# Integer feed-forward layers: exact integer weights, two matmul terms for three, and three steps on other engines

## What is computed

```python
SCALE = 1.0 / 127.0
w = w_int.astype(float32) * SCALE        # w_gate, w_up: 384 x 128, w_down: 128 x 384, integers -127..127
g, u = xn @ w_gate.T, xn @ w_up.T
x = x + (silu(g) * u) @ w_down.T
```

## Time and profile before

| | |
|---|---|
| Runs | 4287.07, 4288.15, 4292.68 us; median 4288.15 |
| Profiled execution | 4286.97 us; span of the records 4285.2 us |
| ffn5 stage: start of the weights' DMA to end of the last statistics | 3685.7 to 3776.2, 90.5 us |
| ffn7 stage, the same | 4183.5 to 4273.8, 90.4 us |
| Busy in the ffn7 stage | TensorE matmuls 66.8, VectorE 62.0, ScalarE 33.9, GpSimd 0.0 us |
| Mean granted TensorE clock in either stage | 0.88 |

### The profile page before, as it was taken

The page is one execution under the profiler, slowest core; times in us unless marked ns, Lnnn a source line. Parts: engine busy times, 40 slices in busy tenths (PEclk is TensorE's granted clock), DMA queues, the critical chain, the costliest instruction groups (busy, mean ns, idle before and its releaser), DMA issues. The chain is left out here.

```text
span 4285.2 us, 58306 instructions
## 1 busy us (share of the span) xinstructions
PE 3440.0 (80%) x18432; PEld 2108.1 (49%) x18432; DVE 3112.8 (73%) x7125; ACT 2445.8 (57%) x4454; POOL 1239.0 (29%) x855
## 2 busy tenths in 40 slices
PE   5788888687946999999999978793499999657736
PEld 2455555365733555555555536572366666433314
DVE  3899999656864777777777745685388887569986
ACT  2788888535722656556565534572299999322203
POOL 0000000034421566666566654341000000025520
PEclk9899999878976999999999988896799999778868
DMA  5333332212436666666766611342634342100000
GB/s 184 60 62 62 62 51 35 37 42 102 143 97 81 86 87 89 85 85 87 90 85 86 84 23 46 112 142 67 189 45 61 60 64 31 26 18 8 5 29 26
DMA packets 285571, 303.79 MB, mean 71 GB/s; under 512 B 97951, under 2 KB 187487, under 8 KB 285140
## 3 DMA queue, kind: packets, MB, share of 16 engines
q1 hardware_dynamic: 275540, 279.07, 37.0%
q0 software_dynamic: 9728, 20.99, 1.4%
HBM read 122.30 MB, written 75.96 MB: 46 GB/s over the span
## 5 line engine op out<-in xcount | busy, mean ns | idle before, releaser
L1118 DVE TENSOR_REDUCE at_b_top<-ps 128x1 f32<-128x512 f32 x1024 | 661.9, 680 | 356.9 <-PE ps L878 356.2
L1007 ACT ACTIVATE at_b_e<-ps 128x512 f32<-128x512 f32 x1024 | 583.6, 598 | 474.2 <-PE ps L884 461.2
L550 ACT ACTIVATE at_a_e<-at_a_logits,at_a_neg_top 128x512 f32<-128x512 f32 x1024 | 656.1, 716 | 156.1 <-DVE at_a_neg_top L610 155.0
L777 POOL TENSOR_TENSOR at_b_e_pair<-at_b_e 128x1024 f32<-128x1024 f32 x256 | 603.8, 2380 | 402.5 <-PE ps L906 400.0
L474 PE MATMUL ps<-at_a_k,at_a_q 96*128 96x512 f32 x1024 | 476.3, 491 | 187.4 <-DVE at_a_clipped L578 118.3
L878 PE MATMUL ps<-at_b_k,at_b_q 96*128 96x512 f32 x1024 | 502.0, 494 | 40.2 <-DMA at_b_k<-at_b_k_hi 37.9
L543 ACT ACTIVATE at_a_eT<-ps 128x512 f32<-128x512 f32 x896 | 461.9, 589 | 0.4
L884 PE MATMUL ps<-at_b_q,at_b_k 98*128 98x512 f32 x1024 | 427.2, 418 | 19.0 <-ACT at_b_e L1007 18.6
L606 DVE CUSTOM_DVE_ANT_0 at_a_logits<-ps,at_a_strip 128x512 f32<-128x512 f32 x512 | 340.3, 688 | 110.7 <-issue 33.1
L474 PEld LDWEIGHTS ps<-at_a_k,at_a_q 96*128 96x128 f32 x1024 | 184.7, 190 | 399.8 <-DVE at_a_clipped L578 208.8
L578 DVE TENSOR_SCALAR at_a_clipped<-ps 128x512 f32<-128x512 f32 x512 | 351.2, 686 | 39.1 <-PE ps L474 38.0
(11 more groups left out here) (333 smaller groups left out, 6451.5 us busy)
## 6 DMA issues: line engine op xcount, KB each, us to landing
moe_stage<-in_moe_w SPq DMA_DIRECT2D x46, 768.0 KB
at_b_q<-at_b_q_hi SPq DMA_DIRECT2D x128, 256.0 KB, 5.2
at_b_k<-at_b_k_hi SPq DMA_DIRECT2D x128, 256.0 KB, 7.7
v<-in_a_va SPq DMA_DIRECT2D x64, 256.0 KB, 3.6
at_a_v<-v SPq DMA_DIRECT2D x64, 256.0 KB, 7.2
at_b_q<-at_b_q_lo SPq DMA_DIRECT2D x64, 256.0 KB, 7.6
at_b_k<-at_b_k_lo SPq DMA_DIRECT2D x64, 256.0 KB, 8.0
slot_rows<-empty_slots SPq DMA_DIRECT2D x44, 288.0 KB, 7.0
```

The source lines that it names most:

```text
L550: act.activation(e[:, j, qb, :], logits[:, j % 2, qb, :], ACT.Exp, bias=neg_top[:, j % 2, qb:qb + 1]).then_inc(exp_done, 1)
L777: pool.tensor_tensor(e_pair[:, j, :, :], e[r][:, j, 0:2, :], e[r][:, j, 2:4, :], ALU.add).then_inc(pair_done, 1)
L1007: act.activation(e[r][:, j, b, :], g.ps[:, ST_BANK + b % 2, :], ACT.Exp).then_inc(exp_done, 1)
L1118: dve.tensor_reduce(top[:, t, j, qb:qb + 1], g.ps[:, bank, :], AX_X, ALU.max).then_inc(max_done, 1)
```

## The change

`swiglu` becomes `integer_swiglu`, for these two layers alone.

- Weights: the integers, converted to float32 and rounded to float32r, which holds them exactly; no w_lo. Each product takes two matmuls (w on high, w on low), not three.
- 1/127 goes on results: as the scale of Silu, as the scalar of the multiply that makes h, as the scale of the acc copy.
- Normalising moves from VectorE to ScalarE, as x * rstd + shift, with shift = -mean * rstd computed once on VectorE (as `linear_attention` does, L1397 and L1491). In step s it comes last, for batch s+1.
- The acc copy moves from VectorE to ScalarE, at q = 2 as before.
- h_lo of chunk 1 moves from VectorE to GpSimd; chunks 0 and 2 stay.
- The turns of x and of the result get PSUM banks of their own (0 and 1); the turn of x waits for x_lo of the batch before, no longer for `out_added`.

TensorE's order stays. The core of the diff:

```diff
-def swiglu(nc, g, name, packed, E, C, stats, router=None):
+def integer_swiglu(nc, g, name, packed, stats):
...
-                def three(bank, w0, cols, hi, lo, start, stop):
-
-                    pe.matmul(bank, w_hi[:, w0, cols], hi, start=start, stop=False)
-                    pe.matmul(bank, w_lo[:, w0, cols], hi, start=False, stop=False)
-                    return pe.matmul(bank, w_hi[:, w0, cols], lo, start=False, stop=stop)
+                def two(bank, cols, hi, lo, start, stop):
+
+                    pe.matmul(bank, w[:, cols], hi, start=start, stop=False)
+                    return pe.matmul(bank, w[:, cols], lo, start=False, stop=stop)
...
+                def turn_x(n):
+                    pe.wait_ge(xn_done, TB * n)
+                    wait(pe, x_lo_done, n - 1)
...
+                for s in range(1, B + 4):
+                    if inside(s - 1):
+                        pe.wait_ge(x_lo_done, s - 1)
+                        if s - 1 == 1:
+                            pe.wait_ge(w_done, 1)
+                    for q in range(C):
+                        if inside(s - 1):
+                            gate_up(s - 1, q)
+                        n, c = (s - 1, q - 2) if q >= 2 else (s - 2, q + 1)
+                        if inside(n):
+                            down(n, c)
+                        if q == 1 and inside(s):
+                            turn_x(s)
+                        if q == 0 and inside(s - 3):
+                            turn_out(s - 3)
...
+                def normalise_on_act(n):
+                    wait(act, xp_ready, n - 1)
+                    for tb in range(TB):
+                        t = (n - 1) * TB + tb
+                        act.activation(xn[:, tb, :], g.x_all[:, t, :], ACT.Identity, bias=shift[:, t:t + 1],
+                                       scale=g.rstd[:, t:t + 1]).then_inc(xn_done, 1)
+
+                act.wait_ge(shift_done, 1)
+                normalise_on_act(1)
+                act.wait_ge(w_float, 1)
+                act.activation(w[:], stage_f[:], ACT.Copy).then_inc(w_done, 1)
+                for s in range(1, B + 4):
+                    for q in range(C):
+                        if inside(s - 1):
+                            m = nth(s - 1, q)
                             act.wait_ge(gu_ready, m)
                             wait(act, h_done, m - 2)
+                            act.activation(gate[:, m % 2, :], g.ps[:, G_BANK + m % 2, :], ACT.Silu, scale=SCALE
+                                           ).then_inc(gate_done, 1)
+                        n, c = previous(s, q)
+                        if inside(n):
+                            act.wait_ge(h_done, nth(n, c))
+                            wait(act, down_done, nth(n - 1, c))
+                            act.activation(h_hi[:, c, :], h[:, c, :], ACT.Copy).then_inc(h_hi_done, 1)
+                        if q == 1 and inside(s):
+                            act.wait_ge(xp_ready, s)
+                            wait(act, gu_ready, C * (s - 2))
+                            act.activation(x_hi[s % 2][:], g.ps[:, X_BANK, :], ACT.Copy).then_inc(x_hi_done, 1)
+                        if q == 2 and inside(s - 2):
+                            act.wait_ge(down_done, C * (s - 2))
+                            wait(act, out_ready, s - 3)
+                            act.activation(acc[:], g.ps[:, D_BANK + s % 2, :], ACT.Copy, scale=SCALE).then_inc(acc_done, 1)
+                        if q == 2 and s < B:
+                            normalise_on_act(s + 1)
+
+            @block.gpsimd
+            def _(pool):
+                for n in range(1, B + 1):
+                    pool.wait_ge(h_hi_done, nth(n, 1))
+                    pool.tensor_tensor(h_lo[:, 1, :], h[:, 1, :], h_hi[:, 1, :].bitcast(F32), ALU.subtract
+                                       ).then_inc(h_lo1_done, 1)
...
+                            dve.scalar_tensor_tensor(h[:, q, :], g.ps[:, U_BANK + m % 2, :], SCALE, gate[:, m % 2, :],
+                                                     ALU.mult, ALU.mult).then_inc(h_done, 1)
+                        n, c = previous(s, q)
+                        if inside(n) and c != 1:
+                            dve.wait_ge(h_hi_done, nth(n, c))
+                            dve.tensor_tensor(h_lo[:, c, :], h[:, c, :], h_hi[:, c, :].bitcast(F32), ALU.subtract
+                                              ).then_inc(h_lo_done, 1)
```

More of the change, by code:

```diff
@@ L1730, in _ @@
                         dve.tensor_tensor(x, x, yn[:, (b - 1) % 2, :, :], ALU.add).then_inc(added, 1)
-def swiglu(nc, g, name, packed, E, C, stats, router=None):
-    EC = E * C
+def integer_swiglu(nc, g, name, packed, stats):
+    C = HID // P
     W = 3 * C * P
[L1741 to L1746, removed]
+    SCALE = float(np.float32(1.0 / 127.0))
     with Phase(nc, name) as ph:
[L1748 to L1751, removed]
+        stage = ph.sb("stage", [P, W], I32)
+        stage_f = ph.sb("stage_f", [P, W])
+        w = ph.sb("w", [P, W], F32R)
+        shift = ph.sb("shift", [P, TILES])
         xn = ph.sb("xn", [P, TB, DM])
-        xT = ph.sb("xT", [P, S])
         x_hi = [ph.sb(f"x_hi{r}", [P, S], F32R) for r in range(2)]
@@ L1768, in swiglu @@
[L1768 to L1797, removed]
@@ new lines, in integer_swiglu, with nth, inside, previous @@
+        out_ready, out_added, stats_done = (ph.sem(k) for k in ("out_ready", "out_added", "stats_done"))
+        X_BANK, OUT_BANK, G_BANK, U_BANK, D_BANK = 0, 1, 2, 4, 6
+        def nth(n, c):
+            return C * (n - 1) + c + 1
+        def inside(n):
+            return 1 <= n <= B
+        def previous(s, q):
+            return (s - 1, q - 1) if q else (s - 2, C - 1)
+        def wait_low(eng, n, c):
+            if c == 1:
+                wait(eng, h_lo1_done, n)
+            else:
+                wait(eng, h_lo_done, 2 * (n - 1) + (1 if c == 0 else 2))
@@ L1831, in _ @@
[L1831 to L1841, removed]
+                sp.dma_start(stage[:], packed[0]).then_inc(w_loaded, 16)
@@ L1855, in gate_up @@
+                def gate_up(n, c):
+                    m, r = nth(n, c), n % 2
                     wait(pe, gate_done, m - 2)
                     wait(pe, h_done, m - 2)
[L1857 to L1866, removed]
-                    if c == 0:
[L1868 to L1871, removed]
@@ L1927, in _, with down @@
-                run_steps(pe, B, 3, step, U=2)
+                    two(g.ps[:, G_BANK + m % 2, :], slice(c * P, (c + 1) * P), x_hi[r][:], x_lo[r][:], True, True)
+                    two(g.ps[:, U_BANK + m % 2, :], slice((C + c) * P, (C + c + 1) * P), x_hi[r][:], x_lo[r][:],
+                        True, True).then_inc(gu_ready, 1)
+                def down(n, c):
+                    wait_low(pe, n, c)
+                    if c == 0:
+                        wait(pe, acc_done, n - 2)
+                    two(g.ps[:, D_BANK + n % 2, :], slice((2 * C + c) * P, (2 * C + c + 1) * P), h_hi[:, c, :],
+                        h_lo[:, c, :], c == 0, c == C - 1).then_inc(down_done, 1)
@@ new lines, in turn_x, with turn_out @@
+                def turn_x(n):
+                    pe.wait_ge(xn_done, TB * n)
+                    wait(pe, x_lo_done, n - 1)
+                    for tb in range(TB):
+                        ins = pe.transpose(g.ps[:, X_BANK, tb * P:(tb + 1) * P], xn[:, tb, :], g.ident[:])
+                    ins.then_inc(xp_ready, 1)
+                def turn_out(n):
+                    pe.wait_ge(acc_done, n)
+                    wait(pe, out_added, n - 1)
+                    for tb in range(TB):
+                        ins = pe.transpose(g.ps[:, OUT_BANK, tb * P:(tb + 1) * P], acc[:, tb * P:(tb + 1) * P], g.ident[:])
+                    ins.then_inc(out_ready, 1)
```

257 lines of the change are left out of this document (30 added, 227 removed).

## The result

The changed kernel takes 4243.91 us (4236.86 to 4245.00, four runs), the one before 4288.2: ratio of the runs 0.9891 (the two medians alone give 0.9897), 95% interval 0.9874 to 0.9908. The direction was right, the size 1.4 times the forecast.

A forecast was written before the change was run, and what follows sets the result against it. No engine full; a loop of waits through VectorE's queue sets the pace. Stage 7.3 + 11.2 + 40.0 + 16.1 = 74.6 us for 90.4; both stages save 31.6, so 4288.15 - 31.6 = 4256.6 us, range 4245 to 4271.

The forecast's parts named there:

- The loop of the steady step: Silu, h_hi, acc, four normalisings, next Silu, h, h_lo, down matmuls, turn of x, gate and up: 7.2 us a step.
- Start: Stage start, weights' DMA to first matmul: 10.3 us becomes 7.3.
- the rival of the table: ScalarE: normalising function not in Silu's table, loads of 1.28 us on the loop, 4298.7 us in all; chance 0.03.
- the two prices: GpSimd's subtraction: 1.27 us, taken, or 2.19 beside VectorE's scans on SBUF tiles, making its loop 6.5 or 7.45 us.
- three low stretches: TensorE's clock in the six steps of a stage: three drops instead of two, each 1.3 us, +3.9 us.
- the rival to which I gave 0.15: Steady steps: loop faster than the sum, no low stretch of the clock at all, 4248.8 us; chance 0.15.
- the end: From the eighth turn of x to the end of the last statistics: 16.1 us for 17.1.
- first steps: From the first matmul to the third turn of x: 12.6 us becomes 11.2.
- the five steps: Third to eighth turn of x: 36.1 us, with the clock 40.0, for 50.4.
- Clock lost for good: TensorE falls to 1.2 GHz throughout, about 9.2 us a step, each stage saves 4.7, 4278.8 us; chance 0.10.
- GpSimd meeting VectorE: GpSimd's subtraction takes 2.19 us, VectorE's h_lo stretches: +0.25 to +0.75 on twelve steps, 4259.6 to 4265.6 us; chance 0.15.

The follow-up runs named there:

- the split: Changed kernel with ScalarE's four normalisings split, two at the end of a step and two behind h_hi at q = 0 of the next: 4227.81 us, ratio 0.9876 to before.
- two terms alone: Kernel before with the matmul on the weights' low half left out of each product, w_lo still formed: steps 9.06 us at the full clock.
- spread_gaps: Changed kernel with four spare 128x512 copies a step added on ScalarE, results unused: steps 7.73 us behind a first of 8.3.
- split_norm_no_gpsimd: Changed kernel with the four normalisings split over two steps and h_lo of chunk 1 back on VectorE: ratio 0.9878 to the kernel before, stages 64.7 and 64.5 us.
- banks_alone: Kernel before with only separate PSUM banks for the turns of x and of the result, and their waits: ffn7 stage 77.8 us, ffn5 78.3.
- undo_two_terms: Changed kernel with w_lo (zero here) formed again and the third matmul back in each product: steps 7.89 us, ffn7 stage 76.3, ffn5 77.7.
- undo_banks: Changed kernel with both turns in one PSUM bank and the turn of x waiting for the addition to x, done ahead of x_lo: ffn7 stage 78.0 us.

## Why the prediction was off

**Right, with its size.** The loop of the steady step: 7.19 against 7.12 us measured, through the very instructions named. It held under eight edits, to 0.1 us in the steps named: 6.6 (6.65 measured) without acc, 6.5 (6.54) without normalising, 6.53 (6.50) and 6.35 (6.36 in the first steps) with the split, 7.8 (7.89) with three matmuls, 8.9 (8.9) with one bank, 9.1 (9.06) for two terms alone, 7.1 (7.12) without GpSimd. It missed spread_gaps by 0.4 and the later steps of split_norm_no_gpsimd by 0.15, where another loop took over; for banks_alone it gave only a range. Start: 7.3 against 6.9 in ffn7; the conversion of the weights began 0.4 sooner after their issue (3.64 against 4.09 us). That is scatter and not the change: over all profiles it took 3.6 to 4.8 us, and in ffn5 the start took 7.4. Silu of chunk 0 follows the fourth normalising with no gap. GpSimd, Silu's table and the length of a normalising, from the line view and the view by groups:

```profile
L1858 ACT ACTIVATE ffn_gate<-ps x48: 577/597/599, 3699.7 to 4224.8; 128x512 f32<-128x512 f32 x48
L1858 ACT ACT_TABLE_LOAD  x2: 1283/1283/1283, 3698.3 to 4171.5; - x2
```

```profile
L1845 ACT ACTIVATE ffn_xn<-x_all,ffn_shift,rstd 128x128 f32<-128x128 f32 x32 | 13.1, 485 | 61.3 <-DVE ffn_shift L1885 61.3
L1880 POOL TENSOR_TENSOR ffn_h_lo<-ffn_h,ffn_h_hi 128x512 fp32r<-128x512 f32 x8 | 10.2, 1273 | 119.1 <-ACT ffn_h_hi L1864 119.1
```

Normalising 485 ns each. One table load a stage: the rival of the table is out, and the rule that the prediction took from the Trainium skill (ScalarE: Activation LUTs, Table sets: the hidden batching unit) agrees with the trace. GpSimd's subtraction takes 1273 ns, the lower of the two prices in the earlier trace rows, and VectorE's h_lo keeps its 0.68 us, so the two didn't meet in the changed kernel. By the Trainium skill (SBUF — State Buffer, Who interferes with whom) a VectorE instruction with two SBUF inputs contends with a GpSimd instruction that reads SBUF. The trace agrees as far as it goes: while GpSimd's subtraction runs at the lower price (4205.73 to 4207.01), VectorE has h and the statistics, each with one SBUF input, and its next h_lo starts at 4208.79. In the drain of undo_two_terms the two do meet, once a stage and for 0.3 us: VectorE's h_lo takes 0.85 us there instead of 0.68, GpSimd's its 1.27. TensorE's waits in the ffn7 stage are the loop's own:

```profile
PE ps L1791 <- POOL ffn_h_lo L1880: 7.2, 8, 1.2
PE ps L1791 <- DVE ffn_x_lo L1904: 3.8, 1, 3.8
PE ps L1791 <- DVE ffn_h_lo L1900: 2.8, 7, 0.6
```

**Wrong: the clock.** I charged three low stretches a stage at 1.3 us, 3.9 us, 7.8 in all. None came: third to eighth turn 35.6 us, which is 5 x 7.12. The step that failed is "I take three low stretches in the six steps instead of two". It rested on the share of matmuls in a step, and spread_gaps shows that this share can fall below that of the kernel before with the clock at 1.00. The rows held the other reading: the fall in the earlier trace rows stood behind a gap of 1.97 us ahead of the turn, and the change removes just that wait. I had seen the gap shrink, and let one gap of 2.01 us without a fall talk me out of it. banks_alone shows it from the one side (the wait gone, clock 1.00 from the third turn), undo_banks from the other (the wait back, 0.94). The longest gap in a step is 0.87 us now, not the 1.2 I worked out. With no low stretch my sum is 4248.8, the rival to which I gave 0.15; the 4.9 us from there to the measured time are, but for a tenth, the terms that follow.

**Mis-sized: the end.** I put 16.1 us from the eighth turn to the end; it is 14.8. The normalising is issued only for `s < B`, so behind step 7 there is none, and the first Silu of step 9 follows acc after 0.7 us, not the 2.0 of the steps before: 1.3 us earlier than my loop has it. I had applied the steady loop one step too far. From the eighth turn to the end of the last Silu lie 8.2 us, not 9.2, and 6.5 from there to the end, not 6.9. Start 0.4, first steps 0.3 and the five steps 0.5 (0.07 a step, and a tenth that I had added to the first) make the rest. Sum per stage: 3.9 + 1.3 + 0.4 + 0.3 + 0.5 = 6.4 of the 6.4 us missed.

**Outside the stages.** Two stages gained 22.3 + 22.2 = 44.5 us, the profiled executions differ by 42.0. ffn5 began 4.4 us later (3690.1 for 3685.7) and from its end to ffn7's start passed 405.5 us for 407.3. Nothing was changed there; over all profiles ffn5's start spreads by 19 us, more than any single edit here but the banks' two stages is worth. My range had no term for it. So it is luck that the gain of the medians, 44.3 us, matches that of the two stages to 0.2.

**Clock lost for good, GpSimd meeting VectorE**: neither occurred.

**What the parts are worth**, in the ffn7 stage and in this order: banks 12.6 alone, 9.9 at the end; two terms 3.4 alone, 8.2 at the end; normalising on ScalarE -0.4 (ffn5 +1.6), h_lo on GpSimd 0.0, acc on ScalarE -1.8 (ffn5 -0.5). The gain is that of the wait and of the matmuls, and each needs the other: the matmuls hide behind the wait while it is there. Two of the three moves named in the change put work on the one queue that came to set the step.

## To carry to other kernels

Write down the loop of the steady step from start-to-start distances and go round it again with the edits in: it gave the step to 0.1 us in the changed kernel and in eight of the ten others, in one of them for the first two steps only. When an edit removes TensorE's longest gap, the clock lost behind that gap comes back too, so look where the falls stand before charging any. Work moved to an idle engine costs up to its full length if it lands between two links of the loop (acc: 0.47 of its 0.49 us a step), until another loop takes over (normalising: 0.6 of 1.55). What falls into the queue's idle places costs less, as the split shows.

## What was unexpected of the hardware

- TensorE's clock fell to 1.2 GHz at or just behind turns with a gap of 1.6 us ahead of them, in 4 of 10, as often as with 2.0 us, and in 7 of 10 with 2.2 us; in steps whose gaps were 0.9 us or shorter (once 1.1) at none of 110. In three of 28 drains it fell behind a gap of 1.2 us, in a fourth behind shorter ones that followed one of 1.3.
- The same code, up to ffn5, took different times in the profiles: 3675.3 to 3679.9 us in four that ran together, 3686.7 to 3688.6 in four others, 3684.5 to 3694.3 in the last four. Nothing here tells why.
